# Four stacked layers on one core: fetched matrices signalled by quarters, two steps moved, the last block's FFN in other banks

## What is computed

```python
x = x + L0(x, itok_B_0_2)        # softmax pooling over tokens, mask by row
x = x + L1(x, ..., condB_uprev)  # attention, 16 heads of 8, sparse or dense bias by row
x = x + L2(x, itok_B_0_7)        # FFN 128 -> 512 -> 128 with relu, low-rank expert (8) by row
x = x + L3(x, itok_B_0_15)       # FFN 128 -> 512 (exact gelu) -> 96 shared + 32 expert (16) columns
```

## Time and profile before

| what | us |
| --- | --- |
| median of 3 runs | 303.71 |
| lowest and highest run | 302.12, 305.19 |
| profiled execution, device time | 302.6 |
| its span, first to last instruction | 300.7 |
| TensorE matmul busy in the span | 259.4 (86%) |
| VectorE, ScalarE, GpSimd busy | 197.9, 134.2, 104.7 |
| mean granted TensorE clock | 0.983 of full |

### The profile page before, as it was taken

How to read it: one execution, slowest core, us unless ns; L and a number is a source line. 1 busy time by engine, 2 the same in 40 slices (tenths; PEclk the granted TensorE clock), 3 DMA queues, 4 the chain that set the end, 5 groups by cost and what they waited for, 6 DMA issues and landing times.

```text
span 300.7 us, 13957 instructions
## 1 busy us (share of the span) xinstructions
PE 259.4 (86%) x5498; PEld 190.2 (63%) x5498; DVE 197.9 (66%) x402; ACT 134.2 (45%) x244; POOL 104.7 (35%) x199
## 2 busy tenths in 40 slices
PE   0099999768899999999999999999999999869565
PEld 0056355545767776777677767776777776648544
DVE  3936887797169857985798579857985796260030
ACT  3042642445057436743674367436743673341131
POOL 6042952055031632163216321632163226212310
PEclk9999999798799999999999999999999999999999
DMA  6979624677087607860876077608760685087401
GB/s 171 351 149 218 180 72 142 208 206 223 3 236 230 205 5 234 221 211 0 231 226 207 0 233 225 205 3 235 221 204 0 186 243 170 11 216 230 145 2 37
DMA packets 35522, 48.82 MB, mean 162 GB/s; under 512 B 11153, under 2 KB 15505, under 8 KB 35362
## 3 DMA queue, kind: packets, MB, share of 16 engines
q1 hardware_dynamic: 35490, 48.38, 56.7%
HBM read 44.17 MB, written 4.19 MB: 161 GB/s over the span
## 4 chain that ended last, share of the span: by engine, by line
PE 62%; SPq 11%; DVE 11%; DMA 7%; issue 6%; ACT 3%; DVEq 0%
PE pB L679 11%; PE pB L713 6%; PE pB L641 6%; PE pB L637 6%; PE pS L611 5%; SPq L260 5%; PE pB L638 5%; SPq L261 5%; DMA ffn_s<-ffn_w_dram 4%; DVE x_l L1072 3%; PE pV L627 3%; PE pB L749 3%; PE pA L571 2%; DMA rw<-w_d 2%; PE pB L750 2%
## 5 line engine op out<-in xcount | busy, mean ns | idle before, releaser
L347 POOL COPY rw<-e3t_s 128x128 f32 x128 | 37.5, 294 | 58.2 <-issue 42.1
L321 POOL TENSOR_TENSOR sc<-sc,rmax 128x512 f32<-128x512 f32 x32 | 33.6, 1049 | 60.4 <-DVE rmax L1019 60.3
L679 PE MATMUL pB<-rw,hT 128*32 128x128 f32 x1024 | 32.5, 283 | 7.9 <-DMA rw<-w_d 5.6
L439 ACT ACTIVATE ex<-sc 128x512 f32<-128x512 f32 x32 | 20.1, 628 | 34.7 <-POOL sc L321 34.7
L679 PEld LDWEIGHTS pB<-rw,hT 128*32 128x32 f32 x1024 | 28.9, 114 | 9.7 <-DMA rw<-w_d 6.1
L713 PE MATMUL pB<-rw,hT 128*32 128x128 f32 x1024 | 34.0, 275 | 0.5 <-ACT hT L447 0.4
L443 ACT ACTIVATE hT<-pB 128x512 f32<-128x512 f32 x32 | 19.0, 595 | 25.9 <-PE pB L641 25.9
L713 PEld LDWEIGHTS pB<-rw,hT 128*32 128x32 f32 x1024 | 26.8, 110 | 4.6 <-issue 3.9
L637 PE MATMUL pB<-x_h,ffn_h 128*128 128x512 f32 x56 | 25.7, 459 | 3.5 <-DVE x_h L1070 2.5
L1025 DVE STREAM_TRANSPOSE pt<-ex 128x512 f32<-128x512 f32 x32 | 22.6, 706 | 7.3 <-ACT ex L439 7.3
L611 PE MATMUL pS<-kb,qs 32*32 32x128 f32 x1024 | 21.6, 276 | 5.1 <-DVE sc L1016 4.6
(11 more groups left out here) (134 smaller groups left out, 492.6 us busy)
## 6 DMA issues: line engine op xcount, KB each, us to landing
rw<-w_d SPq DMA_DIRECT2D x128, 256.0 KB, 3.0
rw<-fc2t_dram SPq DMA_DIRECT2D x4, 768.0 KB, 13.9
xT<-xt_dram SPq DMA_DIRECT2D x8, 256.0 KB, 2.7
xN<-xn_dram SPq DMA_DIRECT2D x8, 256.0 KB, 2.6
w_d<-rw SPq DMA_DIRECT2D x4, 512.0 KB, 3.5
out_dram<-o_s SPq DMA_DIRECT2D x8, 256.0 KB, 3.0
e3t_s<-e3t_dram SPq DMA_DIRECT2D x1, 1024.0 KB, 11.6
ffn_s<-ffn_w_dram SPq DMA_DIRECT2D x1, 896.0 KB, 11.2
```

The source lines that it names most:

```text
L321: pool.tensor_tensor(sc[:, g % 2, :, :], sc[:, g % 2, :, :], rmax[:, g % 2, :].unsqueeze(2).to_broadcast([P, H, S]), ALU.subtract).then_in ...
L347: pool.tensor_copy(rw[:, r, :, SHARED:D], e3t_s[:, bass.ds(e, 1), :, :].rearrange("p o c n -> p (o c) n"))\
L679: last = mm(pB2[S * q:S * q + S, P * g:P * g + P], hid[:, c, tok], rw2[:, Q4 * g + q, c, :], start=(c == 0), stop=(c == FC - 1))
```

## The change

1. **Quarters.** `ld_rw2` becomes four semaphores, one for each group of four rows. `out2(i, g)` raises `ffo_ps` after every group and waits for its own quarter; the fetch of quarter g of the next block waits for `out2(i-1, g)` alone. `final(i, g)` raises `fin_ps` after every group, and GpSimd's copies wait by quarter. Within `out2(i, 0)` the chunks 2 and 3 wait for relu 2 and 3 themselves; the start waits for relu 0 and 1.
2. **Part 0 of the pooling weights** moves on VectorE from behind `score_max(n, 0)` to behind `score_max(n, 3)`; on ScalarE its exponential moves behind `relu(n-1, 0)`.
3. **The bias on x3** (`biased_x3` on GpSimd) waits for x_l (`x3l_sb`) instead of x3.
4. **Step 7 and the tail.** Block 7's attention output is taken behind `out2(6, 0)`; x2 of block 7 is formed in the place of x1 before x3 of block 6; `low(7)` and `hidden(7, 0)` run ahead of `fc1(6)`; the other hidden parts of block 7 run in the banks of attention (pA1, pA0, pV, pA1), with their relus in `kb`, before `token_major(6)` and `final(6)`; `out2(7)` (bank pB1, output in `qs`) stands between `final(6, 1)` and `final(6, 2)`, its turning between `final(6, 2)` and `final(6, 3)`. The groups of `final(7)` go to four banks, and each is summed and stored by itself.

```diff
+        FIN_T = [pB2, pV, pA1, pB1]
+        GIN_T = [pB1[:, :], pA0[:, :], pS0, pS1]
...
-            def expert_weights2(i):
+            def expert_weights2(i, g):
-                at(sp, ffo_ps, i)
-                for r in range(ROWS):
+                at(sp, ffo_ps, G * (i - 1) + g + 1)
+                for r in range(Q4 * g, Q4 * g + Q4):
...
-            store(NBLK - 1)
-            sp.wait_ge(st_out, 16 * (NBLK + 1))
+            for g in range(G):
+                sp.wait_ge(res_sb, NBLK + g)
+                sp.dma_start(out[NBLK - 1, :, g, :], o_s[:, g, :]).then_inc(st_out, 16)
+            sp.wait_ge(st_out, 16 * (NBLK + G))
...
             def biased_x3(i):
-                at(pool, x3_sb, 2 * i + 1)
+                at(pool, x3l_sb, i + 1)
...
             def expert_weights(i, first, last):
-                if first == 0:
-                    at(pool, fin_ps, i + 1)
                 for r in range(first, last):
+                    if r % Q4 == 0:
+                        at(pool, fin_ps, G * i + r // Q4 + 1)
...
                 exps(n, 0)
-                if next_block:
-                    l0_exps(n + 1)
                 exps(n, 1)
                 exps(n, 2)
                 relu(n - 1, 0)
+                if next_block:
+                    l0_exps(n + 1)
                 relu(n - 1, 1)
...
+            for c in range(FC):
+                relu(NBLK - 1, c, (pA1, pA0, pV, pA1), hid_t)
             token_major(NBLK - 2)
+            ffn_out(NBLK - 1, pB1, ffo_t)
             for c in range(FC):
-                relu(NBLK - 1, c)
-            ffn_out(NBLK - 1)
-            for c in range(FC):
-                gelu(NBLK - 1, c)
+                gelu(NBLK - 1, c, GIN_T)
...
-            def out2(i, g):
+            def out2(i, g, ps=pB2, of=hid):
+                at(pe, ld_rw2[g], 16 * Q4 * (i + 1))
                 if g == 0:
-                    at(pe, ld_rw2, 16 * ROWS * (i + 1))
-                    at(pe, hid_sb, FC * (i + 1))
+                    at(pe, hid_sb, FC * i + 2)
                 for c in range(FC):
+                    if g == 0 and c >= 2:
+                        at(pe, hid_sb, FC * i + c + 1)
...
-                if g == G - 1:
-                    last.then_inc(ffo_ps, 1)
+                last.then_inc(ffo_ps, 1)
...
                 out2(n - 1, 0)
+                if not next_block:
+                    attn_out(n)
                 out2(n - 1, 1)
                 out2(n - 1, 2)
                 if next_block:
                     pooling(n + 1)
                 out2(n - 1, 3)
-                attn_out(n)
+                if next_block:
+                    attn_out(n)
+                else:
+                    low(n, pA0)
                 out2_turned(n - 1)
...
+                else:
+                    hidden(n, 0, TAIL)
                 for c in range(FC):
                     fc1(n - 1, c)
...
-            low(NBLK - 1)
+            hidden_expert(NBLK - 1, 0, TAIL)
+            for c in range(1, FC):
+                hidden(NBLK - 1, c, TAIL)
+                hidden_expert(NBLK - 1, c, TAIL)
             token_major(NBLK - 2)
+            final(NBLK - 2, 0)
+            final(NBLK - 2, 1)
             for g in range(G):
-                final(NBLK - 2, g)
+                out2(NBLK - 1, g, pB1, hid_t)
+            final(NBLK - 2, 2)
+            out2_turned(NBLK - 1, ffo_t)
+            final(NBLK - 2, 3)
             for c in range(FC):
-                hidden(NBLK - 1, c)
-                hidden_expert(NBLK - 1, c)
+                fc1(NBLK - 1, c, GIN_T)
+            token_major(NBLK - 1)
+            pe.wait_ge(res_sb, NBLK - 1)
             for g in range(G):
-                out2(NBLK - 1, g)
-            out2_turned(NBLK - 1)
-            for c in range(FC):
-                fc1(NBLK - 1, c)
-            token_major(NBLK - 1)
-            for g in range(G):
-                final(NBLK - 1, g)
+                final(NBLK - 1, g, FIN_T[g])
...
                 score_max(n, 0)
-                if next_block:
-                    pool_weights(n + 1, 0)
                 score_max(n, 1)
...
                 score_max(n, 3)
+                if next_block:
+                    pool_weights(n + 1, 0)
                 turn(n, 2)
...
-            mask_low(NBLK - 1)
+            mask_low(NBLK - 1, pA0)
             result(NBLK - 2)
-            x3(NBLK - 1)
-            result(NBLK - 1)
+            x3(NBLK - 1, x1T)
+            dve.wait_ge(x3n_sb, NBLK)
+            for g in range(G):
+                dve.wait_ge(fin_ps, G * NBLK + g + 1)
+                if g == 0:
+                    dve.wait_ge(st_out, 16 * NBLK)
+                tt(o_s[:, g, :], FIN_T[g][:, P * g:P * g + P], x3n[:, P * g:P * g + P], ALU.add).then_inc(res_sb, 1)
```

More of the change, by code:

```diff
@@ L199, in cond_resid_kernel @@
         hid_ps, hid_sb = sem("hid_ps"), sem("hid_sb")
-        w2_ps, w2_sb, eob_sb, ids_sb, ld_rw2 = (
-            sem("w2_ps"), sem("w2_sb"), sem("eob_sb"), sem("ids_sb"), sem("ld_rw2"))
+        w2_ps, w2_sb, eob_sb, ids_sb = sem("w2_ps"), sem("w2_sb"), sem("eob_sb"), sem("ids_sb")
+        ld_rw2 = [sem("ld_rw2_%d" % g) for g in range(G)]
         oh_sb, eoa_ps, eoa_sb = sem("oh_sb"), sem("eoa_ps"), sem("eoa_sb")
@@ L439, in exps, with relu, gelu, ffn_out @@
                 act.activation(ex[:, g % 2, :, :], sc[:, g % 2, :, :], ACT.Exp).then_inc(ex_sb, 1)
-            def relu(i, c):
+            def relu(i, c, banks=(pB1, pB2, pB0, pB1), to=hid):
                 at(act, hid_ps, FC * i + c + 1)
-                act.activation(hid[:, c, :], [pB1, pB2, pB0, pB1][c][:, :], ACT.Relu).then_inc(hid_sb, 1)
-            def gelu(i, c):
+                act.activation(to[:, c, :], banks[c][:, :], ACT.Relu).then_inc(hid_sb, 1)
+            def gelu(i, c, banks=GIN):
                 at(act, g_ps, FC * i + c + 1)
-                act.activation(hT[:, c, :], GIN[c], ACT.Gelu,
+                act.activation(hT[:, c, :], banks[c], ACT.Gelu,
                                bias=cols_s[:, C_FC1B + c:C_FC1B + c + 1]).then_inc(g_sb, 1)
[L450 to L454, removed]
+            def ffn_out(i, ps=pB2, to=ffo):
+                at(act, ffo_ps, G * (i + 1))
+                act.activation(to, ps[:, :].rearrange("p (g d) -> p g d", d=D), ACT.Copy).then_inc(ffo_sb, 1)
+            def x2_high(i, x2T=x2T):
                 at(act, x2_sb, i + 1)
@@ L647, in whole, with low, hidden @@
                 return [w[:, :] for w in pair]
-            HID = [pB1, pB2, pB0, pB1]
-            def low(i):
+            HID = (pB1, pB2, pB0, pB1)
+            TAIL = (pA1, pA0, pV, pA1)
+            def low(i, ps=pB0):
                 at(pe, x2h_sb, i + 1)
[L653 to L658, removed]
+                if ps is pB0:
+                    at(pe, x3_sb, 2 * i - 1)
+                parts3(ps[:, :], weight(H_EIA), whole(x2p), True, True, (x2l_sb, i + 1)).then_inc(low_ps, 1)
+            def hidden(i, c, banks=HID):
+                if c == 1 and banks is HID:
                     at(pe, res_sb, i)
-                if c == 2:
+                if c == 2 and banks is HID:
                     at(pe, x3n_sb, i)
@@ L695, in fc1 @@
                     at(pe, sc_sb, G * NBLK if isinstance(i, int) and i == NBLK - 1 else G * (i + 2))
[L696 removed]
+                parts3(banks[c], weight(H_FC1, c), whole(x3p), True, True, (x3l_sb, i + 1)).then_inc(g_ps, 1)
             def token_major(i):
@@ L704, in token_major, with final @@
                 last.then_inc(x3t_ps, 1)
-            def final(i, g):
+            def final(i, g, ps=pB2):
                 if g == 0:
```

68 lines of the change are left out of this document (39 added, 29 removed).

## The result

| | before | after |
| --- | --- | --- |
| median, us (runs) | 303.0 (302.12 to 305.19, 4) | 287.12 (282.98 to 289.63, 4) |
| profiled execution: time, span | 302.6, 300.7 | 286.6, 284.8 |
| mean granted TensorE clock | 0.983 | 0.988 |

The ratio after to before is 0.9403, 95% interval 0.9316 to 0.949; it is taken over the executions of each kernel that lie within 1.5% of its fastest (after: 282.98 and 286.6), while the two medians alone would give 0.948. The prediction was 288.4 us (284.5 to 292.5): right, 1.3 us high.

What follows compares the result with a forecast made beforehand. TensorE was taken as the bound, busy 28.99 of 30.00 us in a full step. Gains of 10.67 before the tail plus 5.1 in it, less 0.5, made 15.3: 302.6 to 287.3, or a 288.4 us median (284.5 to 292.5).

Steps and rivals of the forecast that it cites:

- Quarters of block 0: End of step 1: block 0's product starts without waiting for the last fetched matrix, gaining 2.55 us.
- Clock: Step 1: with the hole gone, block 0's 96 matmuls run at full clock, 1.67 us gained (bounds 0 to 1.67).
- rival (1): Step 1: the clock still falls and the half-clock stretch only moves, giving 290.1 us; chance 0.15.
- (5): Step 1: an earlier stretch below full clock goes too, worth 1.5 us, giving 286.9 us; chance 0.08.
- Relu by chunk: Ahead of a block's first expert product: the last relu is no longer waited for, 0.45 us a block, 2.25 in all.
- Bias behind x_l: First fc1 product: x_l runs faster and its waiting matmul starts sooner, 0.31 us a block, 1.86 in all.
- Pooling part 0: Before scores 2 and 3: shorter waits on VectorE, 0.33 plus 0.06 us a step, 2.34 in steps 1 to 6.
- Added waits and increments: TensorE in 7 blocks: added waits and increments cost 0.5 us (bounds 0 to 2.4).
- Rival (4): TensorE: every satisfied wait drains it, making the kernel slower, 305.4 us at 0.5 us per added wait; chance 0.02.
- Tail: From out2(6,0) to the end: earlier fetches and new order end the span at 295.6 instead of 300.7, 5.1 us gained.
- Rival (2): Full step: VectorE becomes the bound at turn 2 and normalise 0, giving 291.4 us; chance 0.13.
- Rival (3): Blocks 0 and 7: fetched quarters land together, so products wait for all, giving 293.6 us; chance 0.04.

Runs made afterwards that it cites:

- run 1: The changed kernel, but block 0's product waits for all four fetched quarters: median 291.84 us, ratio to before 0.9684.
- run 9: run 7 with block 7's attention product moved behind the second group of block 6's product: median 287.46 us, tail 39.08.
- run 11: run 10 with part 0 of the pooling weights behind normalise 0, its exponential behind exponential 3: median 285.63 us, period 28.604.
- run 12: run 7 once more, no edit: median 285.39 us, ratio to before 0.9512, tail 36.27.
- run 2: The changed kernel, but the bias on x3 waits for x3 again, not x_l: median 290.28 us, period 29.229.
- run 3: The changed kernel, but part 0 of the pooling weights stands behind score maximum 0 again: median 287.33 us, period 29.007.
- run 4: The changed kernel, but a block's product waits for all four relus before it starts: median 291.89 us, period 29.343.
- run 6: The changed kernel with 16 more satisfied waits in each of product groups 1 to 3 of every block: median 289.54 us, period 28.803.
- run 10: run 9 with scaled scores 2 ahead of turn 0 on VectorE, only their row maximum behind it: median 287.55 us, period 29.00.
- run 7: The changed kernel with block 7's x3 ahead of block 6's result and its bias ahead of GpSimd's last four copies: median 285.42 us, tail 36.23.
- run 8: The changed kernel once more, no edit: median 287.84 us, ratio to before 0.95, tail 42.37.
- run 5: The changed kernel, but step 7 and the tail in the order, banks and single store of before: median 287.81 us, tail 39.34.

## Why the prediction was right, point by point

- **Quarters of block 0** (2.55): 2.67 by the two rows (2.95 less 0.28), since the product follows a weigh by 0.28, not 0.40. Run 1 shows the cause.
- **Clock** (1.67, bounds 0 and 1.67): 1.66. The upper end was right; run 1 brings the lower one back. In the profiled execution rival (1) is out, and so is (5): the two earlier stretches below full clock are where they were (55 to 60 and 65 to 70 us, a mean granted clock of 0.66 in each, before and after). But (5) hangs on the execution and not on the change: in the profiles of runs 9, 11 and 12 the second stretch is gone (1.00 from 65 to 70 us), and the fastest of after's four executions, 282.98 us, had a mean granted clock of 1.00.
- **Relu by chunk** (0.45 a block): 0.54. What I mis-sized is the gap that remains: I took 0.40 from a weigh followed by another shape of matmul; it is 0.31.
- **Bias behind x_l** (0.31): 0.42. I counted only to the start of the waiting matmul. The one behind it comes another 0.10 earlier (0.23 behind it; with the bias early again, in run 2, 0.34): a matmul that starts out of a wait also delays its follower.
- **Pooling part 0** (0.33 + 0.06): 0.20. I took 1.01 us from final 2 to scores 2, as at final 0; it is 1.13 in the steps of the loop. (In step 7, which has no part 0, the same pair takes 1.02, so about 0.1 of wait seems to be left in the others, too short for the rows to name.) And scores 3 gained nothing: 1.31 behind final 3 before and after. The rest of that wait hangs on turn 0, which stands before scaled scores 2, and both simply came earlier together with scores 2. In step 1 it gave 0.2 at most: scores 2 and 3 wait 0.94 and 1.25 us where they waited 1.17 and 1.24.
- **Their sum** (1.15) against 1.157 is luck in part: one size was too big by 0.19, two were too small by 0.09 and 0.11. Only runs 2 to 4, one edit each, show it.
- **Added waits and increments** (0.5, bounds 0 and 2.4): nothing. Three groups take 2.83 with a wait and an increment each as they did without, and run 6 adds 48 waits for nothing. Rival (4) is out. By the 26 ns for each increment that the Trainium skill's "TensorE: Matmul & The Clock Gate" (The cost: per-tile semaphore tail) gives, an estimate would have made it 1.2 us; the trace does not show it, perhaps because the increment sits on one matmul in 32 (not tried).
- **Steps 2 and 7** gave 0.47 and 0.48 instead of 1.15 and 0.76. The step that failed is that I let every pass gain the same, with no term for stalls without a wait. Step 2 now has one of 0.56; step 7 has 1.11 where it had 0.56 before, and by the sizes of runs 2 and 4 (0.42 + 0.54 = 0.96) less those 0.55 it should give 0.41. What stands beside these stalls is in the DMA table, which lists a queue of its own for instructions:

```profile
q8 instruction: 22, 0.36, 0.5%
```

Of these 22 packets (16 KB each) the trace of after has six between 86 and 113 us, that is in the first pass, none from 113 to 233, the later passes, and three between 233 and 245, in step 7. One of them ends at 92.36, and the stall ends 1.54 us later; one ends at 240.65, and the stall of step 7 ends 1.51 later. In the nine profiles with a first-pass stall it ends 1.27 to 1.54 us behind the end of such a packet, and in step 7 every stall, that of before too, 1.36 to 1.61 behind one. So TensorE seems to stand for its next instructions. The Trainium skill's "Runtime: NRT & Kernel Launch" (Instruction fetch mechanics) says that an engine's instructions come in blocks over a DMA queue of their own, and that crossing a block is mostly hidden but a taken branch may not be. The trace agrees on the blocks and the queue, and here the crossing is not hidden; it does not show a cost of the branch, since passes 2 to 5 stand behind one and have no stall. That the queue feeds TensorE is inferred, and the place of the instructions was not moved, so the cause is read from traces and not shown by a run.

- **Tail** (38.65 from out2(6,0)): 37.6. The hole before the attention product was 0.58 (predicted 0.6). The mis-sized term is the last fetch: I had it 22.55 us behind out2(6,0); it was 21.76, the landing being 2.85 and not 3.52. From x3(7) to the end of the span it is 11.6 against 11.9. x_l(7) was not held up; the copies of GpSimd beside it were, two of them in 1.18 us in place of about 0.95:

```profile
274.37 0.69 DVE L1098 TENSOR_TENSOR x_l<-x3T,x_h 128x512 fp32r<-128x512 f32 x1
...
274.37 1.18 POOL L358 COPY rw<-e3t_s 128x128 f32 x2 [0.40 <-issue]
```

By "SBUF — State Buffer" of the Trainium skill (Who interferes with whom) the one that issues later stands. The trace agrees that one side stands and the other doesn't; which came later it can't show, as both rows start at 274.37. I had put the price on x_l, and the copies paid it.

- **Rival (2)** did not come, yet was close: run 10 crossed the line with one operation moved. **Rival (3)** is refuted: the product that waits for all quarters stands 2.40 us (run 1), the one that waits for its own does not stand at all.
- **The total** is 1.3 high. The profiled execution is 0.7 under the 287.3: 1.07 by the tail, 0.5 by the waits that cost nothing and 0.15 by block 0 and steps 3 to 6, less 0.68 in step 2, 0.28 in step 7 and 0.13 ahead of weigh 3. The other 0.6 is that the median stands 0.5 above the profiled execution, where I carried over the 1.1 of before.

## What to carry to other kernels

Take the period of a repeated step from the starts of one instruction over several passes, and give each edit a run of its own against it: 0.2 us a step was plain there while executions of the same kernel lay up to 6.7 us apart (282.98 to 289.63). Price a removed wait by the gap that the same pair of instructions leaves in another step, and add what its follower gains. When a waiting operation is brought forward, look at what its engine then does later: a queue with 0.1 us in hand turns the next such edit into a loss. And when the work behind a transfer is moved forward, ask how late that transfer comes in a bad execution: the order that is shorter with a prompt fetch can be the longer one with a late fetch.

## What the runs showed of the hardware that was not expected

- The last of block 7's 16 fetches comes promptly or late. Counted from out2(6,0), which triggers the first of them, it reaches TensorE after 21.66 to 21.89 us in seven profiles (after, runs 1, 3, 4, 7, 10, 12; run 2's is prompt too and not waited for), after 23.43 to 23.61 in four (runs 6, 8, 9, 11) and after 24.53 in run 5. When it is late, a DMA share of 0.02 to 0.09, about one engine's, is still seen 1.5 to 2 us behind the rest. In the four, TensorE waits 2.2 to 2.8 us, and its next 32 matmuls take 1.28 to 1.93 us instead of 1.08 as the granted clock goes to the 1.2 GHz level. This makes 3 to 5 us of tail between executions of like kernels (37.62 and 42.37; 36.23 and 39.08).
- Waiting and half clock are not tied one to one. Ahead of block 7's fc1 TensorE waits 1.88 us in after, 1.94 in run 2 and 1.87 in run 4; in after the clock stays at 1.00 until the last product is done, in runs 2 and 4 it goes to the 1.2 GHz level during fc1 (a matmul of 128x512 in 0.63 us instead of 0.40), and the tails are 39.04 and 39.09 instead of 37.62. Waits of 2.40 and 2.49 us had half clock behind them in step 1 (run 1, before), and the wait of 3.08 us in before's tail had none.
- TensorE's stall without a wait in the loop's first pass is 0.26 to 1.81 us in nine profiles, always inside the last group of `final`, at its 21st matmul or next to it (after and runs 1, 2, 5, 6, 7, 8, 10, 12), and ends 1.27 to 1.54 us behind an instruction packet. Passes 2 to 5 of the loop have neither a stall nor a packet of that queue in any profile.
- GpSimd's sum x3b takes 1.05 us with VectorE's x_l out of its way, and 1.18 beside it.
